# Routing from the logits instead of their exponentials, and layer-norm offsets moved from GpSimd to VectorE

## The chip, the cores and the metric

The kernel runs on one core of one Trainium2 chip. Five engines work in parallel, each through its own queue in order: TensorE (PE in the profile, its weight loads PEld), VectorE (DVE), ScalarE (ACT), GpSimd (POOL) and SyncE (SP), which here only issues DMAs. They wait for each other through semaphores. The metric is the device time of one execution in microseconds.

## What is computed

A transformer block with modulated layer norms (`c`, `wmod`), on 16 batches of 512 tokens with 128 channels: an attention with softmax over each head of q (8 channels) and over the tokens for k, then a mixture of 8 experts of which each token uses 2. Cut to what matters:

```python
h = _layernorm(x) * (1 + ca) + sa
q, k, v = h @ Wq.T + bq, h @ Wk.T + bk, h @ Wv.T + bv
q = softmax(q, axis=-1)            # over the 8 channels of a head
k = softmax(k, axis=-2)            # over the tokens
out = q @ (k.T @ v)                # per head, then a layer norm, Wo, bo
x = x + ga * out
h = _layernorm(x) * (1 + cb) + sb
probs = softmax(h @ router_w)      # 8 experts
top_p, top_e = top_k(probs, 2)
x = x + gb * sum over the two of top_p * (gelu(h @ w_in[e] + b_in[e]) @ w_out[e] + b_out[e])
```

## The kernel before

All five queues are written out by hand, with one loop each over steps b. A step works on several batches at once, at different stages: the experts of batch b+1 (from its second half on; the last ones of batch b before), the attention of b+2, the projections of b+3 and the first layer norm of b+4. In each engine's block a function `step(b)` lists the pieces in their order; a piece starts with the waits for its inputs, and an engine that waits holds up everything behind it. A batch lies in SBUF as 128 partitions by T = 4 tokens by 128 channels. The experts' products `v = u * gate_bc` (`weigh`, 512 columns each) are shared out: experts 1, 3 and 5 to GpSimd, the others to VectorE.

The pieces that matter here, by their lines in the profile:

- First layer norm: `ln1_stats`, `ln1_var` on VectorE give mean and variance (`mv1`), `ve1` (L834) and the negated mean `nm1` (L835). GpSimd's `rstd_L` makes `rstd1` by a power (L328) and the offset `nmr1 = nm1 * rstd1` (L330). ScalarE's `ln1_apply` (L446) uses both. The second norm does the same: L916, L917, L370, L372, and ScalarE's L452 writes `xn2`, which TensorE transposes (L655); ScalarE's L439 and L440 evacuate it to `h2` and `h2_hi`, and GpSimd makes `h2_lo` (L349).
- `k_max`: L839 takes the negated maximum of k over the tokens out of PSUM, L842 makes `kshift` of it and the bias column in `cols`, for ScalarE's exponential (L458).
- `route`: L922 takes the maximum of the 8 logits of each token out of PSUM, L925 subtracts it (`lshift`). ScalarE's `exp_router` (L468) makes `elg`.
- `gates_out`: the two largest of `elg` are found by a maximum (L930) and cut out by a match and replace (L934), 4 times each; `elg - elg_cut` are the chosen ones (L938), times the inverse sum (L936) twice (L943, L944), and the differences (L947). TensorE transposes the result (L666, `gate_turn`); from there it goes over ScalarE (L497) and two DMAs to all partitions as `gate_bc`, for the products.
- VectorE's step ends with `v_bias`, `q_sum` and `route`; the next begins with `q_inv` (L871), `state_out` (`s2T`, L888, after TensorE's L629), `q_norm` (`qn`, L876), `k_inv` and `gates_out`.
- GpSimd's step: `h_low` (L365), `rstd_L`, `rstd_B`, expert 1 (L355), `gated_const` (L334), `residual2` (L359), expert 3, `h2_low` (L349), expert 5, `gated_weight` (L339), `rstd_O` (L344).

Of the kernel before, what the change touches and what calls it, by code (L numbers as in the profile page):

```python
# [27 lines left out]
P = 128  # L28
# [6 lines left out]
def adaln_block(nc, x, Wq, bq, Wk, bk, Wv, bv, Wo, bo, ln_g, ln_b, router_w, w_in, b_in, w_out, b_out, c, wmod, out, gate_scratch, route_scratch):  # L35
# [14 lines left out]
    with ExitStack() as ctx:  # L50
# [3 lines left out]
        def sem(name):  # L54
# [56 lines left out]
        nm1 = sb("nm1", [P, T])  # L111
# [6 lines left out]
        nkmax = sb("nkmax", [P, 1])  # L118
# [23 lines left out]
        nm2 = sb("nm2", [P, T])  # L142
# [6 lines left out]
        lmax = sb("lmax", [P, T])  # L149
        top = sb("top", [P, 4, T, 8])  # L150
        elg_cut = sb("elg_cut", [P, T, NE])
# [3 lines left out]
        einv = sb("einv", [P, T])  # L155
        echosen = sb("echosen", [P, T, NE])
# [29 lines left out]
            "hT_done hhi_ready hlo_ready kT_done kmax_done kshift_ready ek_exp kinv_ready qv_done qb_ready qmax_done qs_ready v_ready "  # L186
# [3 lines left out]
            "h2T_done h2hi_ready h2lo_ready logits_done lmax_done top_done cut_done lshift_ready elg_ready "  # L190
            "esum_done einv_done echosen_done gates_made gate2_ready gateT_done gateT_ready gateTr_ready "
# [106 lines left out]
        def _(pool):  # L298
# [7 lines left out]
            def masks():  # L306
# [8 lines left out]
                pool.memset(top[:, 1:4, :, :], 3.0e38).then_inc(s["const_ready"], 1)  # L315
# [433 lines left out]
        def _(dve):  # L749
# [78 lines left out]
            def ln1_var(n):  # L828
# [81 lines left out]
            def ln2_var(n):  # L910
# [143 lines left out]
```

## Time and profile before

| | before |
|---|---|
| median of 3 runs | 392.79 us (391.56 to 392.8) |
| the profiled execution | 392.8 us, its span 391.1 us |
| TensorE busy | 362.9 us (93%), weight loads 327.3 us (84%) |
| VectorE busy | 282.5 us (72%), 1060 instructions |
| ScalarE busy | 278.5 us (71%) |
| GpSimd busy | 216.8 us (55%), 221 instructions |

The span is the time from the first to the last instruction of the profile. Shares of busy time are averages over all steps; what an operation is worth is read from the waits and from the timelines of one step, which repeats 14 times nearly unchanged. In a timeline row the second number is the duration of the instruction; "xN" stands for N of a kind in a row, merged.

### The profile page before, as it was taken

How to read it: one execution, taken by the hardware profiler on the slowest of the kernel's cores; microseconds unless marked ns; L12 is line 12 of the kernel's file. 1: busy time of each engine (PE TensorE's matmuls, PEld its weight loads, DVE VectorE, ACT ScalarE, POOL GpSimd, SP SyncE). 2: the span in 40 equal slices, each digit the busy share in tenths (PEclk: the TensorE clock that was granted, in tenths of full speed). 3: DMA queues.
4: the chain of work that ended last, by engine and by line, in shares of the span. 5: the costliest groups of instructions: out<-in, count | busy, mean ns of one | idle time of the engine just before them, and what ended most of it. 6: DMA issues, size and time to landing. Idle time of an engine off the chain costs nothing.

```text
span 391.1 us, 8091 instructions
## 1 busy us (share of the span) xinstructions
PE 362.9 (93%) x2502; PEld 327.3 (84%) x2502; DVE 282.5 (72%) x1060; ACT 278.5 (71%) x502; POOL 216.8 (55%) x221
## 2 busy tenths in 40 slices
PE   3657789999999999999999999999999999999995
PEld 3446679889999999899899999898998999988875
DVE  2665586787777888878877778788788787786432
ACT  3333679688787969696887879696969878675740
POOL 2315447373938466483838384664837383754543
PEclk9966579999999999999999999999999999999999
DMA  5570051240706071321606070605224150605061
GB/s 182 151 297 2 0 173 73 80 193 24 247 5 242 29 225 47 157 115 41 231 33 241 3 244 27 240 32 168 106 104 169 38 208 3 217 28 216 32 227 41
DMA packets 18817, 47.83 MB, mean 122 GB/s; under 512 B 2571, under 2 KB 6102, under 8 KB 18518
## 3 DMA queue, kind: packets, MB, share of 16 engines
q1 hardware_dynamic: 18576, 46.90, 33.3%
q8 instruction: 20, 0.33, 0.3%
q10 hardware_dynamic: 198, 0.41, 0.3%
q14 instruction: 23, 0.19, 0.1%
HBM read 42.82 MB, written 4.48 MB: 121 GB/s over the span
## 4 chain that ended last, share of the span: by engine, by line
PE 66%; DVE 9%; issue 6%; DMA 6%; POOL 5%; SPq 4%; ACT 2%; POOLq 0%; DVEq 0%; ACTq 0%
PE pY L684 19%; PE pH L672 6%; PE pH L674 6%; PE pH L673 6%; PE pB L661 4%; PE pQV L641 4%; PE pC L629 4%; PE pC L648 3%; POOL v L355 2%; DVE qn L876 2%; DMA gate_bc<-route_scratch 2%; DMA gates<-gate_scratch 2%; SPq L236 2%; DVE elg_cut L934 2%; PE pA L588 2%
## 5 line engine op out<-in xcount | busy, mean ns | idle before, releaser
L684 PE MATMUL pY<-wout,v 128*128 128x128 f32 x1024 | 128.7, 277 | 1.0 <-DVE v L958 0.7
L684 PEld LDWEIGHTS pY<-wout,v 128*128 128x128 f32 x1024 | 121.7, 193 | 2.2 <-DVE v L958 1.1
L502 ACT ACTIVATE u<-pH,cols 128x512 f32<-128x512 f32 x128 | 86.4, 689 | 49.5 <-PE pH L674 42.8
L344 POOL TENSOR_TENSOR rstd_o<-ve_o,neg_half 128x4 f32<-128x4 f32 x16 | 22.0, 1376 | 104.3 <-DVE ve_o L895 104.3
L958 DVE TENSOR_TENSOR v<-u,gate_bc 128x512 f32<-128x512 f32 x80 | 68.6, 860 | 7.0 <-DMA gate_bc<-route_scratch 3.7
L355 POOL TENSOR_TENSOR v<-u,gate_bc 128x512 f32<-128x512 f32 x48 | 63.7, 1329 | 9.0 <-DMA gate_bc<-route_scratch 9.0
L672 PE MATMUL pH<-h_hi,win_hi 128*128 128x512 f32 x128 | 54.9, 429 | 1.4 <-ACT u L502 1.4
L673 PE MATMUL pH<-h_hi,win_lo 128*128 128x512 f32 x128 | 50.6, 395 | 0.0
L674 PE MATMUL pH<-h_lo,win_hi 128*128 128x512 f32 x128 | 50.5, 394 | 0.0
L349 POOL TENSOR_TENSOR h_lo<-h,h_hi 128x512 fp32r<-128x512 f32 x16 | 22.5, 1405 | 20.2 <-ACT h_hi L440 20.2
L452 ACT ACTIVATE xn<-x_all,nmr,rstd 128x128 f32<-128x128 f32 x64 | 26.2, 482 | 4.5 <-POOL nmr L372 4.5
L847 DVE TENSOR_TENSOR qs<-pQV,bq_bc 128x512 f32<-128x512 f32 x16 | 11.1, 692 | 25.1 <-PE pQV L607 25.1
L672 PEld LDWEIGHTS pH<-h_hi,win_hi 128*128 128x128 f32 x128 | 24.3, 190 | 5.8 <-issue 2.4
L674 PEld LDWEIGHTS pH<-h_lo,win_hi 128*128 128x128 f32 x128 | 24.2, 189 | 5.7
L673 PEld LDWEIGHTS pH<-h_hi,win_lo 128*128 128x128 f32 x128 | 24.4, 190 | 3.4
L446 ACT ACTIVATE xn<-x_all,nmr,rstd 128x128 f32<-128x128 f32 x64 | 26.3, 494 | 0.0
L365 POOL TENSOR_TENSOR h_lo<-h,h_hi 128x512 fp32r<-128x512 f32 x16 | 20.4, 1274 | 8.4 <-ACT h_hi L432 8.4
L902 DVE SCALAR_TENSOR_TENSOR x_all<-pC,rstd_o,x_all 128x128 f32<-128x128 f32 x64 | 18.0, 345 | 8.6 <-PE pC L648 6.7
L359 POOL TENSOR_TENSOR x_all<-x_all,yg 128x512 f32<-128x512 f32 x16 | 21.3, 1332 | 4.4 <-DVE yg L963 4.4
L334 POOL TENSOR_TENSOR x_all<-x_all,gates 128x512 f32<-128x512 f32 x16 | 20.6, 1285 | 5.3 <-DMA gates<-gate_scratch 5.3
L370 POOL TENSOR_TENSOR rstd<-ve,neg_half 128x4 f32<-128x4 f32 x16 | 16.5, 1031 | 10.8 <-DVE nm L917 10.8
L629 PE MATMUL pC<-ek,v_sb 128*128 128x128 f32 x128 | 18.9, 295 | 2.9 <-ACT ek L473 2.9
(151 smaller groups left out, 781.5 us busy)
## 6 DMA issues: line engine op xcount, KB each, us to landing
gate_bc<-route_scratch SPq DMA_DIRECT2D x64, 512.0 KB, 5.7
x_all<-in_L_attn_x SPq DMA_DIRECT2D x16, 256.0 KB, 6.9
out<-x_all SPq DMA_DIRECT2D x16, 256.0 KB, 2.0
gates<-gate_scratch SPq DMA_DIRECT2D x1, 2048.0 KB, 7.1
gb_bc<-gb_scratch SPq DMA_DIRECT2D x1, 1024.0 KB, 4.6
route_scratch<-gateT SPq DMA_DIRECT2D x64, 4.0 KB
win<-in_L_ffn_w_in SPq DMA_DIRECT2D x1, 512.0 KB, 5.6
wout<-in_L_ffn_w_out SPq DMA_DIRECT2D x1, 512.0 KB, 6.9
```

What stands on the lines that cost most here:

```text
L344: pool.tensor_tensor(rstd_o[:, :], ve_o[:, :], neg_half[:, :], ALU.pow).then_inc(s["rstdo_ready"], 1)
L349: pool.tensor_tensor(h2_lo[:, n % 2, :], h2[:, :], h2_hi[:, n % 2, :].bitcast(F32), ALU.subtract).then_inc(s["h2lo_ready"], 1)
L355: pool.tensor_tensor(v[:, e % U, :], u[:, e % U, :], gate_bc[:, b % 2, e, :], ALU.mult).then_inc(s["vp_done"], 1)
L446: act.activation(xn1[:, t, :], x_all[:, n, t, :], ACT.Identity, bias=nmr1[:, t:t + 1], scale=rstd1[:, t:t + 1]).then_inc(s["xn1_ready"], 1)
L452: act.activation(xn2[:, t, :], x_all[:, n, t, :], ACT.Identity, bias=nmr2[:, t:t + 1], scale=rstd2[:, t:t + 1]).then_inc(s["xn2_ready"], 1)
L502: act.activation(u[:, e % U, :], pH[:, e % 2, :], ACT.Gelu_apprx_tanh, bias=cols[:, e:e + 1]).then_inc(s["gelu_done"], 1)
L629: i = mm(pS, v_sb[:, t, :], ek[:, t, :], start=(t == 0), stop=(t == T - 1))
L672: mm(o, win_hi[:, e, :], h2_hi[:, b % 2, :], start=True, stop=False)
L673: mm(o, win_lo[:, e, :], h2_hi[:, b % 2, :], start=False, stop=False)
L674: mm(o, win_hi[:, e, :], h2_lo[:, b % 2, :], start=False, stop=True).then_inc(s["mm1_done"], 1)
L684: i = mm(pY[:, t * P:(t + 1) * P], v[:, e % U, t * P:(t + 1) * P], wout[:, e, :], start=False, stop=(e == NE - 1), skip_group_check=True)
L958: dve.tensor_tensor(v[:, e % U, :], u[:, e % U, :], gate_bc[:, b % 2, e, :], ALU.mult).then_inc(s["v_done"], 1)
```

## The change

Four edits.

1. `k_max`: the maximum is taken without negation, then `kbmax = kmax + bias` and `kshift = bias - kbmax`, two additions of [P, 1] SBUF columns in place of one operation.
2. Layer-norm offsets: `nm1`, `nm2` and GpSimd's two products are gone. VectorE makes `nmr = -mean * rstd` by one operation with two SBUF inputs, in new pieces `ln2_offset` and `ln1_offset`, each behind a wait for GpSimd's rstd.
3. `route` now copies the logits from PSUM to `lg`, takes the 8 sorted values of each token from PSUM (`top`), copies the first two to `top2` (the other six of which hold 3e38), subtracts the largest, and cuts the two largest out of `lg` (`lg_cut`).
4. `gates_out` compares `lg` with `lg_cut` (`chosen`), multiplies by `elg`, then by the inverse sum; the rounded gate is a copy of the gate instead of a second product.

```diff
             def route(n):
                 dve.wait_ge(s["logits_done"], n + 1)
-                logits = pB[:, 0:T * NE].rearrange("p (t e) -> p t e", e=NE)
-                dve.tensor_reduce(lmax[:, :], logits, AX.X, ALU.max).then_inc(s["lmax_done"], 1)
-                dve.wait_ge(s["lmax_done"], n + 1)
-                w(dve, "elg_ready", n)
-                dve.tensor_tensor(lshift[:, :, :], logits, lmax[:, :].unsqueeze(2).to_broadcast([P, T, NE]), ALU.subtract).then_inc(s["lshift_ready"], 1)
+                dve.tensor_copy(lg[:, :, :].rearrange("p t e -> p (t e)"), pB[:, 0:T * NE]).then_inc(s["lg_ready"], 1)
+                for t in range(T):
+                    dve.max(top[:, t, :], pB[:, t * NE:(t + 1) * NE]).then_inc(s["top_done"], 1)
+                dve.wait_ge(s["top_done"], T * n + T)
+                dve.tensor_copy(top2[:, :, 0:2], top[:, :, 0:2]).then_inc(s["top2_done"], 1)
+                dve.wait_ge(s["lg_ready"], n + 1)
+                dve.wait_ge(s["top2_done"], n + 1)
+                dve.tensor_tensor(lshift[:, :, :], lg[:, :, :], top[:, :, 0:1].to_broadcast([P, T, NE]),
+                                  ALU.subtract).then_inc(s["lshift_ready"], 1)
+                for t in range(T):
+                    dve.match_replace(lg_cut[:, t, :], top2[:, t, :], lg[:, t, :], -3.0e38).then_inc(s["cut_done"], 1)
 
             def gates_out(n):
+                dve.wait_ge(s["cut_done"], T * n + T)
+                dve.tensor_tensor(chosen[:, :, :], lg[:, :, :], lg_cut[:, :, :], ALU.not_equal).then_inc(s["chosen_done"], 1)
                 dve.wait_ge(s["elg_ready"], n + 1)
-                for t in range(T):
-                    dve.max(top[:, 0, t, :], elg[:, t, :]).then_inc(s["top_done"], 1)
                 dve.tensor_reduce(esum[:, :], elg[:, :, :], AX.X, ALU.add).then_inc(s["esum_done"], 1)
-                for t in range(T):
-                    dve.wait_ge(s["top_done"], T * n + t + 1)
-                    dve.match_replace(elg_cut[:, t, :], top[:, :, t, 0:2], elg[:, t, :], 0.0).then_inc(s["cut_done"], 1)
...
             def k_max(n):
                 dve.wait_ge(s["kT_done"], n + 1)
-                dve.tensor_reduce(nkmax[:, :], pA[:, :], AX.X, ALU.max, negate=True).then_inc(s["kmax_done"], 1)
+                dve.tensor_reduce(kmax[:, :], pA[:, :], AX.X, ALU.max).then_inc(s["kmax_done"], 1)
                 dve.wait_ge(s["kmax_done"], n + 1)
+                dve.tensor_tensor(kbmax[:, :], kmax[:, :], cols[:, NE:NE + 1], ALU.add).then_inc(s["kbmax_done"], 1)
+                dve.wait_ge(s["kbmax_done"], n + 1)
                 w(dve, "ek_exp", n)
-                dve.tensor_scalar(kshift[:, :], nkmax[:, :], cols[:, NE:NE + 1], cols[:, NE:NE + 1], ALU.subtract, ALU.add).then_inc(s["kshift_ready"], 1)
+                dve.tensor_tensor(kshift[:, :], cols[:, NE:NE + 1], kbmax[:, :], ALU.subtract).then_inc(s["kshift_ready"], 1)
...
+            def ln2_offset(n):
+                dve.wait_ge(s["rstd2_ready"], n + 1)
+                w(dve, "xn2_ready", T * n)
+                dve.scalar_tensor_tensor(out=nmr2[:, :], in0=mv2[:, :, 0], scalar=-1.0, in1=rstd2[:, :],
+                                         op0=ALU.mult, op1=ALU.mult).then_inc(s["nmr2_ready"], 1)
```

What this does to VectorE's queue, at three places of one step. The first is the end of the step, where the routing stands between `q_sum` and the next step's `q_inv`. Before:

```order
L867 TENSOR_REDUCE qsum<-eq 128x64
L922 TENSOR_REDUCE lmax<-pB 128x4
L925 TENSOR_TENSOR lshift<-pB,lmax 128x32
L871 RECIPROCAL qinv<-qsum 128x64
L888 TENSOR_TENSOR s2T<-pC,blockmask 128x128
```

and now (line numbers in these rows are those of the changed kernel):

```order
L873 TENSOR_REDUCE qsum<-eq 128x64
L933 COPY lg<-pB 128x32
L935 MAX top<-pB 128x8 x4
L938 COPY top2<-top 128x4x2
L941 TENSOR_TENSOR lshift<-lg,top 128x32
L944 MATCH_REPLACE lg_cut<-top2,lg 128x8 x4
L877 RECIPROCAL qinv<-qsum 128x64
L894 TENSOR_TENSOR s2T<-pC,blockmask 128x128
```

Two instructions have become five entries with eleven instructions, and the match work stands ahead of `q_inv` and `s2T`. The second place is `gates_out`, between `k_inv` and the copy of the transposed gates. Before:

```order
L930 MAX top<-elg 128x8 x4
L931 TENSOR_REDUCE esum<-elg 128x4
L934 MATCH_REPLACE elg_cut<-top,elg 128x8 x4
L936 RECIPROCAL einv<-esum 128x4
L938 TENSOR_TENSOR echosen<-elg,elg_cut 128x32
L943 TENSOR_TENSOR gate2<-echosen,einv 128x4x8
L944 TENSOR_TENSOR gate2<-echosen,einv 128x4x8
L947 TENSOR_TENSOR gate2<-gate2 128x4x16
```

and now:

```order
L948 TENSOR_TENSOR chosen<-lg,lg_cut 128x32
L950 TENSOR_REDUCE esum<-elg 128x4
L952 TENSOR_TENSOR echosen<-elg,chosen 128x32
L954 RECIPROCAL einv<-esum 128x4
L957 TENSOR_TENSOR gate2<-echosen,einv 128x4x8
L960 CAST gate2<-gate2 128x4x8
L963 TENSOR_TENSOR gate2<-gate2 128x4x16
```

Maxima and replacements are gone from here. The third place is the middle of the step, behind the second layer norm's variance; `v` are the experts' products. Before:

```order
L917 TENSOR_SCALAR nm2<-mv2 128x4
L963 TENSOR_TENSOR yg<-pY,gb_bc 128x512
L958 TENSOR_TENSOR v<-u,gate_bc 128x512
L839 TENSOR_REDUCE nkmax<-pA 128x1
L842 TENSOR_SCALAR kshift<-nkmax,cols 128x1
L847 TENSOR_TENSOR qs<-pQV,bq_bc 128x512
L858 TENSOR_REDUCE qmax<-qs 128x64
L958 TENSOR_TENSOR v<-u,gate_bc 128x512
L862 TENSOR_TENSOR qs<-qs,qmax 128x512
```

and now:

```order
L979 TENSOR_TENSOR yg<-pY,gb_bc 128x512
L974 TENSOR_TENSOR v<-u,gate_bc 128x512
L927 SCALAR_TENSOR_TENSOR nmr2<-mv2,rstd2 128x4
L842 TENSOR_REDUCE kmax<-pA 128x1
L845 TENSOR_TENSOR kbmax<-kmax,cols 128x1
L848 TENSOR_TENSOR kshift<-cols,kbmax 128x1
L853 TENSOR_TENSOR qs<-pQV,bq_bc 128x512
L864 TENSOR_REDUCE qmax<-qs 128x64
L974 TENSOR_TENSOR v<-u,gate_bc 128x512
L836 SCALAR_TENSOR_TENSOR nmr1<-mv1,rstd1 128x4
L868 TENSOR_TENSOR qs<-qs,qmax 128x512
```

`nm2` is gone, the two offsets and one operation of `k_max` have come in. On GpSimd the two offset products behind the powers are gone and nothing else has moved.

## Rows read from the trace of the kernel before

**Rows 1.** waits, whole run: engine, line, releaser: us in total, times, longest
```profile
PEld pB L666 <- DVE gate L947: 5.8, 15, 0.7
```

**Rows 2.** chain of waits, two periods: start us, us, what
```profile
155.89 0.55 DVE elg_cut L934 x4
...
157.30 0.33 PE pB L666
...
178.75 0.33 PE pB L666
```

**Rows 3.** timeline, VectorE: start us, us, engine, line, op, shapes, [idle before <-releaser]
```profile
153.26 0.19 DVE L925 TENSOR_TENSOR lshift<-pB,lmax 128x32 f32<-128x32 f32 x1
153.37 0.54 DVE L871 RECIPROCAL qinv<-qsum 128x64 f32<-128x64 f32 x1
154.57 0.29 DVE L888 TENSOR_TENSOR s2T<-pC,blockmask 128x128 f32<-128x128 f32 x1 [0.67 <-PE pC L629]
154.78 0.68 DVE L876 TENSOR_TENSOR qn<-eq,qinv 128x512 f32<-128x512 f32 x1
...
155.45 0.35 DVE L930 MAX8 top<-elg 128x8 f32<-128x8 f32 x4
...
157.02 0.22 DVE L947 TENSOR_TENSOR gate<-gate 128x64 f32<-128x64 f32 x1
```

**Rows 4.** timeline, GpSimd, around the same step
```profile
154.25 0.46 POOL L339 TENSOR_TENSOR sw_rhs<-wo_gain,gates 128x128 f32<-128x128 f32 x1
...
165.38 1.01 POOL L370 TENSOR_TENSOR rstd<-ve,neg_half 128x4 f32<-128x4 f32 x1 [0.40 <-DVE nm L917]
...
166.62 1.30 POOL L355 TENSOR_TENSOR v<-u,gate_bc 128x512 f32<-128x512 f32 x1
...
170.35 1.28 POOL L355 TENSOR_TENSOR v<-u,gate_bc 128x512 f32<-128x512 f32 x1
173.07 1.45 POOL L349 TENSOR_TENSOR h_lo<-h,h_hi 128x512 fp32r<-128x512 f32 x1 [1.44 <-ACT h_hi L440]
174.48 1.27 POOL L355 TENSOR_TENSOR v<-u,gate_bc 128x512 f32<-128x512 f32 x1
```

**Rows 5.** timeline, VectorE, later in that step
```profile
165.13 0.17 DVE L917 TENSOR_SCALAR nm<-mv 128x4 f32<-128x4 f32 x1
...
165.80 0.68 DVE L958 TENSOR_TENSOR v<-u,gate_bc 128x512 f32<-128x512 f32 x1
...
169.10 0.69 DVE L847 TENSOR_TENSOR qs<-pQV,bq_bc 128x512 f32<-128x512 f32 x1 [1.71 <-PE pQV L607]
...
170.43 1.75 DVE L958 TENSOR_TENSOR v<-u,gate_bc 128x512 f32<-128x512 f32 x1
```

**Rows 6.** timeline, GpSimd, a late step
```profile
342.43 1.75 POOL L355 TENSOR_TENSOR v<-u,gate_bc 128x512 f32<-128x512 f32 x1
```

**Rows 7.** timeline, VectorE, late steps
```profile
342.94 1.78 DVE L862 TENSOR_TENSOR qs<-qs,qmax 128x512 f32<-128x512 f32 x1
...
359.44 1.29 DVE L958 TENSOR_TENSOR v<-u,gate_bc 128x512 f32<-128x512 f32 x2
```

**Rows 8.** one line, L372: duration ns min/median/max, first and last start us
```profile
L372 POOL TENSOR_TENSOR nmr<-nm,rstd x16: 199/202/686, 37.7 to 360.1; 128x4 f32<-128x4 f32 x16
```

**Rows 9.** timeline, ScalarE, the step of rows 3 to 5
```profile
153.96 0.23 ACT L468 ACTIVATE elg<-lshift 128x32 f32<-128x32 f32 x1
...
167.34 1.64 ACT L452 ACTIVATE xn<-x_all,nmr,rstd 128x128 f32<-128x128 f32 x4
```

**Rows 10.** timeline, VectorE, preparation of the weights
```profile
10.62 0.22 DVE L788 TENSOR_SCALAR sw_rhs<-ident 128x128 f32<-128x128 f32 x1
```

**Rows 11.** timeline, GpSimd, near the start and the end
```profile
37.89 1.27 POOL L334 TENSOR_TENSOR x_all<-x_all,gates 128x512 f32<-128x512 f32 x1
...
366.44 1.27 POOL L355 TENSOR_TENSOR v<-u,gate_bc 128x512 f32<-128x512 f32 x1
```

**Rows 12.** timeline, VectorE, the last routing
```profile
366.29 0.19 DVE L922 TENSOR_REDUCE lmax<-pB 128x4 f32<-128x32 f32 x1 [3.74 <-PE pB L661]
```

More of the change, by code:

```diff
@@ L117, in adaln_block @@
         h_lo = sb("h_lo", [P, NTOK], F32R)
-        nkmax = sb("nkmax", [P, 1])
+        kmax = sb("kmax", [P, 1])
+        kbmax = sb("kbmax", [P, 1])
         kshift = sb("kshift", [P, 1])
@@ L148, in adaln_block @@
         h2_lo = sb("h2_lo", [P, 2, NTOK], F32R)
-        lmax = sb("lmax", [P, T])
-        top = sb("top", [P, 4, T, 8])
-        elg_cut = sb("elg_cut", [P, T, NE])
+        lg = sb("lg", [P, T, NE])
+        top = sb("top", [P, T, 8])
+        top2 = sb("top2", [P, T, 8])
+        lg_cut = sb("lg_cut", [P, T, NE])
         lshift = sb("lshift", [P, T, NE])
@@ L155, in adaln_block @@
         einv = sb("einv", [P, T])
+        chosen = sb("chosen", [P, T, NE])
         echosen = sb("echosen", [P, T, NE])
@@ L314, in masks @@
                                    pattern=[[HEAD_DIM, HEADS], [0, HEAD_DIM]], channel_multiplier=-1).then_inc(s["const_ready"], 1)
-                pool.memset(top[:, 1:4, :, :], 3.0e38).then_inc(s["const_ready"], 1)
+                pool.memset(top2[:, :, :], 3.0e38).then_inc(s["const_ready"], 1)
             def gates_loaded():
@@ L367, in rstd_B @@
             def rstd_B(n):
-                pool.wait_ge(s["ve2_done"], 2 * (n + 1))
+                pool.wait_ge(s["ve2_done"], n + 1)
                 w(pool, "xn2_ready", T * n)
                 pool.tensor_tensor(rstd2[:, :], ve2[:, :], neg_half[:, :], ALU.pow).then_inc(s["rstd2_ready"], 1)
-                pool.wait_ge(s["rstd2_ready"], n + 1)
-                pool.tensor_tensor(nmr2[:, :], nm2[:, :], rstd2[:, :], ALU.mult).then_inc(s["nmr2_ready"], 1)
             def step(b):
@@ L832, in ln1_var, with ln1_offset @@
                 dve.wait_ge(s["mv1_done"], T * n + T)
-                w(dve, "nmr1_ready", n)
+                w(dve, "rstd1_ready", n)
                 dve.tensor_scalar(ve1[:, :], mv1[:, :, 1], LN_EPS, None, ALU.add).then_inc(s["ve1_done"], 1)
-                dve.tensor_scalar(nm1[:, :], mv1[:, :, 0], -1.0, None, ALU.mult).then_inc(s["ve1_done"], 1)
+            def ln1_offset(n):
+                dve.wait_ge(s["rstd1_ready"], n + 1)
+                w(dve, "xn1_ready", T * n)
+                dve.scalar_tensor_tensor(out=nmr1[:, :], in0=mv1[:, :, 0], scalar=-1.0, in1=rstd1[:, :],
+                                         op0=ALU.mult, op1=ALU.mult).then_inc(s["nmr1_ready"], 1)
             def k_max(n):
                 dve.wait_ge(s["kT_done"], n + 1)
-                dve.tensor_reduce(nkmax[:, :], pA[:, :], AX.X, ALU.max, negate=True).then_inc(s["kmax_done"], 1)
+                dve.tensor_reduce(kmax[:, :], pA[:, :], AX.X, ALU.max).then_inc(s["kmax_done"], 1)
                 dve.wait_ge(s["kmax_done"], n + 1)
+                dve.tensor_tensor(kbmax[:, :], kmax[:, :], cols[:, NE:NE + 1], ALU.add).then_inc(s["kbmax_done"], 1)
+                dve.wait_ge(s["kbmax_done"], n + 1)
                 w(dve, "ek_exp", n)
-                dve.tensor_scalar(kshift[:, :], nkmax[:, :], cols[:, NE:NE + 1], cols[:, NE:NE + 1], ALU.subtract, ALU.add).then_inc(s["kshift_ready"], 1)
+                dve.tensor_tensor(kshift[:, :], cols[:, NE:NE + 1], kbmax[:, :], ALU.subtract).then_inc(s["kshift_ready"], 1)
             def q_bias(n):
@@ L931, in gates_out @@
                 dve.tensor_reduce(esum[:, :], elg[:, :, :], AX.X, ALU.add).then_inc(s["esum_done"], 1)
-                for t in range(T):
-                    dve.wait_ge(s["top_done"], T * n + t + 1)
-                    dve.match_replace(elg_cut[:, t, :], top[:, :, t, 0:2], elg[:, t, :], 0.0).then_inc(s["cut_done"], 1)
+                dve.wait_ge(s["chosen_done"], n + 1)
+                dve.tensor_tensor(echosen[:, :, :], elg[:, :, :], chosen[:, :, :], ALU.mult)
                 dve.wait_ge(s["esum_done"], n + 1)
@@ L944, in gates_out @@
-                dve.tensor_tensor(gate2[:, :, 1, :].bitcast(F32R), echosen[:, :, :], spread, ALU.mult).then_inc(s["gates_made"], 1)
-                dve.wait_ge(s["gates_made"], 2 * (n + 1))
+                dve.tensor_tensor(gate2[:, :, 0, :], echosen[:, :, :], einv[:, :].unsqueeze(2).to_broadcast([P, T, NE]),
+                                  ALU.mult).then_inc(s["gate_done"], 1)
+                dve.wait_ge(s["gate_done"], n + 1)
+                dve.tensor_copy(gate2[:, :, 1, :].bitcast(F32R), gate2[:, :, 0, :]).then_inc(s["ghi_done"], 1)
@@ L1007, in step @@
                     weigh(b + 1, 0)
+                if has(b + 2):
+                    ln2_offset(b + 2)
                 if has(b + 3):
@@ L1013, in step @@
                     weigh(b + 1, 2)
+                if has(b + 4):
+                    ln1_offset(b + 4)
                 if b == -4:
```

21 lines of the change are left out of this document (6 added, 15 removed).

## The prediction

> **What bounds the kernel now.** I read the waits of TensorE's weight loads first, since TensorE is busy nearly all the time: one wait recurs in every step. The transpose of the gates (L666) waits for VectorE's last gate operation (L947), 15 times, 5.8 us in all [rows 1], 0.39 us a step. The chain of waits then gives the period: that transpose starts at 157.30 and again at 178.75, 21.45 us apart, and the chain reaches it over VectorE, not over TensorE [rows 2]. So the kernel sits where two chains are almost equally long. What VectorE saves here is worth at most 0.39 us a step, then TensorE alone bounds; every microsecond that VectorE is later at this place costs one.
>
> VectorE's timeline ahead of the transpose shows how little room there is [rows 3]. The routing ends with q's reciprocal at 153.91, VectorE idles 0.67 us for the state matmuls, then come s2T (154.57), qn (154.78) and the gate chain from 155.45 to 157.25, 1.80 us long. Starts in that view also price small operations: the next one starts 0.11 us after the start of a 32-column operation that it does not depend on (153.26 to 153.37), and 0.04 us after the end of one that it does (0.19 + 0.04 = 0.23 us).
>
> GpSimd's timeline is the second to look at, for it is not the bound, but works without a gap twice a step [rows 4]: four 512-column operations from 166.62 to 171.63 (L355, L334, L359, L355), and from 173.07 to 176.2 L349, L355 and L339 (the last shown at 154.25 for 0.46 us, one period earlier).
>
> **The port that both engines use.** The trace shows VectorE and GpSimd keeping each other off when both read two SBUF tensors. VectorE's product at 170.43 takes 1.75 instead of 0.69 us and ends 0.55 us after GpSimd's, begun at 170.35, ends [rows 5]. They take turns: at 342.43 GpSimd waits (1.75 instead of 1.28 us) behind a VectorE product, and VectorE's next two-input operation, issued at 342.94, waits until GpSimd is done (1.78 us) [rows 6, 7]. Smallness does not help: GpSimd's 4-column product L372, 0.20 us in the median, takes 0.69 us when VectorE runs two products [rows 6 to 8]. One exception: VectorE's product at 165.80 is not held up though GpSimd's power operation runs from 165.38 to 166.39 [rows 4, 5].
>
> The Trainium skill (SBUF — State Buffer, section "SBUF: two separate sides") states the rule as an exclusive lock held for the whole instruction, and counts among those who take it VectorE operations with two SBUF inputs or in a two-port mode. The 512-column rows agree; the power operation does not, since VectorE was not kept out for its whole duration. With a lock of that whole length the product at 165.80 would have started after 166.39, which the rows exclude, so I let the power operation hold nothing.
>
> **The change, part by part.**
>
> Gate chain (`gates_out`). Gone from it: four maxima (0.35 with a tail of 0.08 that overlaps [rows 3]: 0.27), the four value loads and replacements (0.55 [rows 2]). New: chosen, and a cast that now depends on gate. After: chosen 0.23 to the dependent echosen, +0.11 until the reciprocal, +0.17+0.04 until gate, +0.23 until the cast, +0.20 until the last, which takes 0.22: 1.20 us against 1.80. That is 0.60 us off the critical chain. GpSimd is idle here, so nothing collides.
>
> Routing (`route`). The match work is not gone, it comes earlier, ahead of s2T and qn. New in front of lshift: a copy out of PSUM (0.09 to 0.11), four maxima (0.27), a copy of two columns of each to top2 (0.12 wait, 0.19); behind lshift four replacements (0.55). lshift was read from PSUM and one SBUF tensor and is now read from two SBUF tensors. It is issued while GpSimd runs its fifth product (174.48 to 175.75 [rows 4]). That is what I hold to be decisive.
>
> Offsets. `nm1`, `nm2` vanish (0.17 us each [rows 5], of which I count 0.08, since the next operation does not wait for their end), GpSimd loses two 4-column products, and VectorE makes both offsets itself after a wait for rstd. Behind the wait of ln2_offset stand k_max, q_bias and the rest of VectorE's step; ScalarE's xn (L452, from 167.34 [rows 9]) waits for the result. The wait itself ends in time: with nm2 gone rstd2 is there at about 166.31 instead of 166.39 and the product ahead of it ends at 166.40 instead of 166.48. But GpSimd needs no semaphore after rstd and starts its first product at about 166.28, to 167.58; the offset, with two SBUF inputs, follows at about 167.65. xn starts 0.36 us later, at 167.70. It has cover: its transpose on TensorE comes at 170.7. The delay passes on to h2_hi, and there to GpSimd's L349, 173.07 + 0.36 = 173.43.
>
> Key maximum. One operation becomes two additions with two SBUF inputs each. Each meets one of GpSimd's gapless operations: 168.35 is put off to 169.05, the second to 170.4. q_bias stood idle until 169.10 [rows 5], so it loses 1.3 us. But the product at 170.43 lost 1.07 us to GpSimd before and is now behind it: it ends at 172.42 instead of 172.18. With ln1_offset (0.12) q_sum ends about 0.36 us later, at 174.94; ln1_offset is used at 173.9, later than it is made (172.5).
>
> **The sum for one step**, in the clock of the rows:
> - L349: issued at 173.43, held up by VectorE's product until about 173.65, ends at 174.90; GpSimd's fifth product then runs from 174.86 to 176.13 (before: to 175.75).
> - Copy out of PSUM 174.87, maxima until 175.30, copy to top2 issued at 175.34. A one-source SBUF operation of 128 columns takes 0.22 us [rows 10], one that reads PSUM 0.29 (L888 [rows 3]). I read the difference as twice the reading pace, so through both ports, and take it that top2's copy does so too and waits, to 176.19.
> - GpSimd's L339 (0.46 us) is next in turn, so lshift ends at 176.66 instead of 174.90.
> - Replacements from 176.60, q's reciprocal 177.15, s2T 177.61, qn 177.82, gate chain 178.49, its end 1.21 later, transpose at 179.75.
>
> Against 178.75 that is +1.0 us a step: +1.6 at qn less 0.60 in the gate chain. ScalarE's exponential follows lshift to 176.9 (it was 175.41, from 153.96 [rows 9]), and sw, qT and gateT behind it stay in front of their users by 0.2 us and more. The delay closes the loop, since all that follows hangs on the transpose; it counts in the 14 intervals from gates 0 to gates 14. To this comes the start: at 37.89 GpSimd begins 1.27 us of work [rows 11], now beside the first ln2_offset, for whose result ScalarE and TensorE wait there, +0.9. And the end: the last lmax starts at 366.29 after an idle wait, and GpSimd's product runs from 366.44 to 367.71 [rows 11, 12]; gates end at about 369.65 instead of 368.81, +0.85. Sum: 14 x 1.0 + 0.9 + 0.85 = 15.75. The profiled execution took 392.8 us (391.1 of span and 1.7 around it), which is the median of the three: 408.5 us.
>
> The Trainium skill's page "VectorE: DVE Perf Modes" (section "Mode 2×_2P — use both read ports for one tensor") says that one-source SBUF operations of 32-bit data read their tensor through both ports; with the exclusive lock of the page above, top2's copy would wait as I assume. No row shows such an operation beside a large GpSimd one, so no row decides it.
>
> **The rivals.**
> - *Only two-input operations wait, top2's copy does not.* lshift waits for the fifth product alone and ends at 176.19; everything behind it is 0.47 us earlier, the step +0.5: 14 x 0.52 + 1.75 = 9.0, 401.8 us. For it: two columns are hardly worth a second port. Against it: the doubled pace in [rows 10].
> - *Small operations slip through (faster than before).* If 1 to 32 columns with two SBUF inputs need no turn, lshift ends at 175.1, the replacements and q's reciprocal end at 176.05, just inside the idle 0.67 us, and qn stays at 176.23. Then the gate chain ends 0.6 us sooner, TensorE's wait goes, and the rest is TensorE's own work: -5.8 [rows 1], 387.0 us. It decides as soon as lshift ends before about 175.6. For it: the old kshift, small and beside GpSimd, never waited, but it has one SBUF tensor. Against it: L372 [rows 8].
> - *In between*: turns are given such that lshift ends near 175.7 and gain and loss cancel, 391.6 to 394.
> - *Worse*: VectorE's products later in the step are caught too, another 0.3 us a step, 413 us.
> - That the moved work is not moved is excluded by the instruction order.
>
> **How the numbers follow.** 0.46 for the forecast (408.5), 0.25 for two-input operations alone (401.8), 0.08 for worse (413), 0.07 for in between, 0.14 for the gain (387.0). The range 399 to 412.5 holds the first two with their errors of 0.15 us a step; the gain and the in-between stay out with 0.2. A measurement of this kernel tells 0.3% (1.2 us) from no change. Slower 0.79, the same 0.07, faster 0.14.
>
> **What would show it.** Right: lshift lasts over 0.5 us instead of 0.19 and ends with GpSimd's product or with L339's successor; top2's copy lasts about 0.9 us; one of kbmax and kshift lasts more than 0.5 us; TensorE's wait for the last gate operation grows from 0.39 to over 1 us a step; the period is near 22.45 us. Wrong: all these small operations last under 0.25 us, and the wait at L666 is gone. The forecast also falls if GpSimd's fifth product does not overlap the routing, or if xn's delay reaches TensorE by another way.

## The result

| | before | changed |
|---|---|---|
| median | 392.68 us (391.56 to 392.8) | 402.55 us (401.06 to 402.87) |
| profiled execution | 392.8 us, span 391.1 | 400.12 us, span 398.1 |
| gates 0 to gates 14 (start of their transposes) | 301.70 us | 309.50 us |
| a usual step | 21.45 us | 22.01 us |
| gates 14 to gates 15 | 17.94 us | 18.89 us |

The changed kernel takes 1.0261 times as long, with an interval of 1.0223 to 1.03: slower by 2.6%, as forecast in sign, 6 us less than forecast. The page of the changed kernel begins:

```profile
span 398.1 us, 8137 instructions
...
PE 360.4 (91%) x2502; PEld 323.7 (81%) x2502; DVE 324.8 (82%) x1108; ACT 281.8 (71%) x502; POOL 207.5 (52%) x189
```

TensorE works as long as before; VectorE's busy share has gone from 72% to 82%. Waiting counts as busy here, as the timelines show.

The waits of the whole run (us in total, times, longest), against [rows 1]:

```profile
ACT elg L465 <- DVE lshift L941: 11.3, 16, 2.1
...
PEld pB L663 <- DVE gate L963: 9.6, 16, 1.0
...
PEld pB L658 <- ACT h_hi L437: 8.0, 15, 0.9
```

The weight load for the gates' transpose waits 9.6 instead of 5.8 us, and two others have grown: ScalarE's exponential for lshift (1.0 us before) and the weight load for the logits, for h2_hi (3.4 us before). TensorE's timeline gives the period, against the 157.30 and 178.75 of [rows 2]:

```profile
158.75 0.33 PE L663 MATMUL pB<-ident,gate 128*128 128x128 f32 x1 [0.36 <-DVE gate L963]
...
180.77 0.33 PE L663 MATMUL pB<-ident,gate 128*128 128x128 f32 x1 [0.37 <-DVE gate L963]
```

VectorE's timeline of one step, from s2T over the gate chain to the next routing (compare [rows 3, 5]; durations in us in the second column):

```profile
156.71 0.22 DVE L894 TENSOR_TENSOR s2T<-pC,blockmask 128x128 f32<-128x128 f32 x1
156.85 0.67 DVE L882 TENSOR_TENSOR qn<-eq,qinv 128x512 f32<-128x512 f32 x1
...
157.52 0.17 DVE L948 TENSOR_TENSOR chosen<-lg,lg_cut 128x32 f32<-128x32 f32 x1
...
158.47 0.23 DVE L963 TENSOR_TENSOR gate<-gate 128x64 f32<-128x64 f32 x1
...
167.81 1.25 DVE L927 SCALAR_TENSOR_TENSOR nmr<-mv,rstd 128x4 f32<-128x4 f32 x1
...
169.69 0.62 DVE L845 TENSOR_TENSOR kbmax<-kmax,cols 128x1 f32<-128x1 f32 x1
170.34 1.20 DVE L848 TENSOR_TENSOR kshift<-cols,kbmax 128x1 f32<-128x1 f32 x1
...
172.77 0.68 DVE L974 TENSOR_TENSOR v<-u,gate_bc 128x512 f32<-128x512 f32 x1
...
176.41 0.93 DVE L938 COPY top<-top 128x8 f32<-128x8 f32 x1
177.45 0.33 DVE L941 TENSOR_TENSOR lshift<-lg,top 128x32 f32<-128x32 f32 x1
```

and GpSimd's beside it (compare [rows 4]):

```profile
167.74 1.30 POOL L354 TENSOR_TENSOR v<-u,gate_bc 128x512 f32<-128x512 f32 x1
169.00 1.29 POOL L333 TENSOR_TENSOR x_all<-x_all,gates 128x512 f32<-128x512 f32 x1
170.25 1.27 POOL L358 TENSOR_TENSOR x_all<-x_all,yg 128x512 f32<-128x512 f32 x1
171.47 1.28 POOL L354 TENSOR_TENSOR v<-u,gate_bc 128x512 f32<-128x512 f32 x1
174.82 1.27 POOL L348 TENSOR_TENSOR h_lo<-h,h_hi 128x512 fp32r<-128x512 f32 x1 [2.06 <-ACT h_hi L437]
176.05 1.27 POOL L354 TENSOR_TENSOR v<-u,gate_bc 128x512 f32<-128x512 f32 x1
177.28 0.46 POOL L338 TENSOR_TENSOR sw_rhs<-wo_gain,gates 128x128 f32<-128x128 f32 x1
```

Read the two together, with the wait counted in the duration of the operation that waits. The second offset (L927) is issued at 167.81, just after GpSimd began its product at 167.74, lasts 1.25 us and ends at 169.06, when that product is over (169.04). kbmax ends at 170.31 with the next one (170.29), kshift at 171.54 with the third (171.52). The copy to top2 (L938), eight elements, lasts 0.93 us and ends at 177.34 with the fifth product (177.32). lshift comes in while L338 runs and ends at 177.78, behind it (177.74). All five of these small operations end within 0.05 us after a GpSimd instruction. The product at 172.77, on the other hand, takes its plain 0.68 us: in [rows 5] it took 1.75, and its GpSimd partner is now over before it.

The gate chain, from L948 (157.52) to the end of L963 (158.70), lasts 1.18 us against 1.80 before. So the change shortens what it set out to shorten, and loses more ahead of it.

### The profile page after: what moved, and what is told of

It reads as the page before. It is cut to its first block, busy times and chain, and to the rows that moved or that the text cites. A ratio compares the mean times of both kernels' runs of the same rounds, so it can differ in the third digit from the quotient of the medians.

```text
span 398.1 us, 8137 instructions
## 1 busy us (share of the span) xinstructions
PE 360.4 (91%) x2502; PEld 323.7 (81%) x2502; DVE 324.8 (82%) x1108; ACT 281.8 (71%) x502; POOL 207.5 (52%) x189
## 4 chain that ended last, share of the span: by engine, by line
issue 41%; POOL 29%; DVE 13%; DMA 9%; SPq 4%; ACT 2%; POOLq 1%; PE 1%; DVEq 0%; ACTq 0%
POOL v L354 11%; DMA gate_bc<-route_scratch 4%; POOL x_all L333 4%; POOL x_all L358 3%; POOL h_lo L364 3%; POOL rstd_o L343 2%; DMA route_scratch<-gateT 2%; POOL rstd L329 2%; DMA gates<-gate_scratch 2%; SPq L237 2%; DVE nmr L927 1%; POOL rstd L369 1%; DVE x_all L908 1%; POOL sw_rhs L338 1%; DVE v L974 1%
## 5 line engine op out<-in xcount | busy, mean ns | idle before, releaser
L974 DVE TENSOR_TENSOR v<-u,gate_bc 128x512 f32<-128x512 f32 x80 | 57.7, 723 | 4.8 <-DMA gate_bc<-route_scratch 3.4
L348 POOL TENSOR_TENSOR h_lo<-h,h_hi 128x512 fp32r<-128x512 f32 x16 | 20.3, 1272 | 30.8 <-ACT h_hi L437 30.8
L364 POOL TENSOR_TENSOR h_lo<-h,h_hi 128x512 fp32r<-128x512 f32 x16 | 20.4, 1274 | 8.9 <-ACT h_hi L429 8.9
L658 PEld LDWEIGHTS pB<-rw,h 128*128 128x128 f32 x128 | 16.3, 199 | 9.9 <-ACT h_hi L437 8.0
L333 POOL TENSOR_TENSOR x_all<-x_all,gates 128x512 f32<-128x512 f32 x16 | 20.6, 1286 | 5.6 <-DMA gates<-gate_scratch 5.6
L658 PE MATMUL pB<-rw,h 128*128 128x8 f32 x128 | 17.7, 265 | 5.9 <-ACT h_hi L437 5.8
```

The lines of the kernel that those rows point to most:

```text
L333: pool.tensor_tensor(x_all[:, n, :, :], x_all[:, n, :, :], gates[:, n, 1, :].unsqueeze(1).to_broadcast([P, T, P]), ALU.add).then_inc(s["xg ...
L364: pool.tensor_tensor(h_lo[:, :], h[:, :], h_hi[:, :].bitcast(F32), ALU.subtract).then_inc(s["hlo_ready"], 1)
L658: i = mm(pB[:, t * NE:(t + 1) * NE], h2[:, t * P:(t + 1) * P], rw[:, :], start=True, stop=True)
L974: dve.tensor_tensor(v[:, e % U, :], u[:, e % U, :], gate_bc[:, b % 2, e, :], ALU.mult).then_inc(s["v_done"], 1)
```

## The experiments

Three explanations stood against each other. Theory P: small VectorE operations that need the second way into SBUF (two SBUF inputs, or a copy that reads through two ports) wait for the running GpSimd operation. Theory W: it is the work itself, moved and added ahead of qn. Theory O: it is the offsets, whose wait for rstd puts VectorE behind GpSimd. "Step" below is the usual distance between the gates' transposes. The ratio is to runs of the kernel before on the same chip, with a 95% interval; the runs were made on several chips, on which the kernel before had medians of 392.68 to 392.91 us.

| run | median us | ratio to before | step us |
|---|---|---|---|
| kernel before | 392.68 | 1 | 21.45 |
| changed kernel | 402.55 | 1.0261 (1.0223 to 1.03) | 22.01 |
| a1, routing alone | 399.39 | 1.0145 (1.0108 to 1.0182) | 21.9 |
| a2, offsets alone | 398.06 | 1.012 (1.0084 to 1.0155) | 21.76 |
| a3, k_max alone | 391.17 | 0.9963 (0.9936 to 0.9989) | 21.45 |
| d2, k_max alone again | 392.18 | 0.9987 (0.9973 to 1.0002) | 21.45 |
| a4, changed, routing clear of the port | 393.58 | 1.0027 (0.9995 to 1.0059) | 21.43 |
| b1, clear routing alone | 388.56 | 0.9892 (0.9873 to 0.991) | 21.16 |
| b2, changed, lshift from PSUM | 399.36 | 1.0166 (1.0146 to 1.0187) | 21.86 |
| b3, changed, no copy | 396.49 | 1.0093 (1.0073 to 1.0113) | 21.59 |
| c1, probes (one execution) | 392.75 | | 21.45 |
| d1, clear routing and k_max | 387.39 | 0.9864 (0.9846 to 0.9881) | 21.14 |

**a1, the edits of route and gates_out alone.** The kernel before with the routing of the diff and nothing else of it:

```diff
+                dve.tensor_copy(top2[:, :, 0:2], top[:, :, 0:2]).then_inc(s["top2_done"], 1)
...
+                dve.tensor_tensor(lshift[:, :, :], lg[:, :, :], top[:, :, 0:1].to_broadcast([P, T, NE]), ALU.subtract)
```

> The kernel before with the edits of route and gates_out alone. Theory P (small VectorE operations with two SBUF inputs, or with a two-port copy, wait for GpSimd's running operation): the copy to top2 lasts about 0.8 us and lshift about 0.4 us beside GpSimd's fifth product, the step takes 21.9 instead of 21.45 us, in all +7.5 us, 400 us. Theory W (it is the added and moved work itself, no waiting for GpSimd): copy and lshift last 0.15 to 0.2 us each, the routing is about 0.7 us longer than before, the gate chain 0.6 us shorter, the step within 0.2 us of before, 389 to 395 us. Theory O (the offsets cause the loss, by the wait for rstd): as before or a little faster, 388 to 393 us.

Measured 399.39 us. The two operations in question, over the whole run (min/median/max in ns), and the transposes:

```profile
L928 DVE COPY top<-top x16: 219/768/930, 45.5 to 373.3; 128x8 f32<-128x8 f32 x16
...
L931 DVE TENSOR_TENSOR lshift<-lg,top x16: 191/330/338, 45.8 to 374.3; 128x32 f32<-128x32 f32 x16
```

```profile
159.86 0.33 PE L668 MATMUL pB<-ident,gate 128*128 128x128 f32 x1 [0.46 <-DVE gate L953]
...
181.73 0.33 PE L668 MATMUL pB<-ident,gate 128*128 128x128 f32 x1 [0.46 <-DVE gate L953]
```

The copy lasts 0.77 us in the median, less than in the changed kernel, since it comes in 0.53 us after the start of GpSimd's product (177.55 against 177.02) instead of 0.36: it lasts what is left of it. The time is P's; W would have it at 389 to 395 us, O at 388 to 393.

**a2, the offsets alone.**

```diff
+                dve.scalar_tensor_tensor(out=nmr2[:, :], in0=mv2[:, :, 0], scalar=-1.0, in1=rstd2[:, :],
+                                         op0=ALU.mult, op1=ALU.mult).then_inc(s["nmr2_ready"], 1)
...
-                pool.tensor_tensor(nmr2[:, :], nm2[:, :], rstd2[:, :], ALU.mult).then_inc(s["nmr2_ready"], 1)
```

> The kernel before with the edit of the layer-norm offsets alone. Theory P: the second offset waits for GpSimd's first product (about 1.2 us), ScalarE's xn comes 0.3 us later, and the logits on TensorE with it; since the state matmuls stand behind them, the gate chain comes 0.3 us later: +4 us and under 1 us at the start, about 397 us. Theory W: unchanged within 0.3%. Theory O: nearly the whole loss of the change, 400 us or more.

Measured 398.06 us; the second offset and the transposes:

```profile
L921 DVE SCALAR_TENSOR_TENSOR nmr<-mv,rstd x16: 1212/1249/1259, 37.5 to 366.6; 128x4 f32<-128x4 f32 x16
```

```profile
160.65 0.33 PE L660 MATMUL pB<-ident,gate 128*128 128x128 f32 x1
...
182.40 0.33 PE L660 MATMUL pB<-ident,gate 128*128 128x128 f32 x1
```

A 4-column operation (the first offset, the same operation with no GpSimd instruction beside it, takes 0.15 us in the changed kernel) lasts 1.25 us in every step. The step is 21.75 us, 0.3 longer, as expected; some steps took 22.1 or 22.65, which makes the sum 1 us larger than expected. P's 397 us is the nearest; W (unchanged) and O (400 us or more) are both off. The edit by itself accounts for 5 us, and the routing by itself for 6.5, together for more than the 9.9 of both. In steps: on top of the new routing the offsets cost only 0.11 us (a1 to the changed kernel), not 0.3. The rows show where it goes. Without the offsets GpSimd's h2_low (L351 in a1) comes early enough to meet VectorE's product and lasts 1.44 us; with them it starts 0.31 us later (16.07 instead of 15.76 behind the gates' transpose), when that product is over, and lasts 1.27, so the fifth product ends only 0.14 us later. In a1:

```profile
175.62 1.44 POOL L351 TENSOR_TENSOR h_lo<-h,h_hi 128x512 fp32r<-128x512 f32 x1 [1.45 <-ACT h_hi L442]
```

**a3 and d2, k_max alone.**

```diff
+                dve.tensor_tensor(kbmax[:, :], kmax[:, :], cols[:, NE:NE + 1], ALU.add).then_inc(s["kbmax_done"], 1)
+                dve.wait_ge(s["kbmax_done"], n + 1)
...
+                dve.tensor_tensor(kshift[:, :], cols[:, NE:NE + 1], kbmax[:, :], ALU.subtract).then_inc(s["kshift_ready"], 1)
```

> The kernel before with the edit of k_max alone. Theory P: kbmax and kshift each wait for one of GpSimd's gapless operations (over 0.5 us and over 1 us), but VectorE idled 1.7 us behind them until q_bias, so the time stays within 0.3% of before, 392 to 394 us. Theory W: the same time, but both last under 0.25 us. Theory O: the same as W.

```profile
L843 DVE TENSOR_TENSOR kbmax<-kmax,cols x16: 159/794/801, 18.6 to 338.3; 128x1 f32<-128x1 f32 x16
L846 DVE TENSOR_TENSOR kshift<-cols,kbmax x16: 159/1214/1218, 18.9 to 339.2; 128x1 f32<-128x1 f32 x16
```

Two additions of one column each: 0.79 and 1.21 us in the median, 0.16 in the shortest case. Two microseconds of VectorE's time a step, and the kernel is not slower, since q_bias behind them waited until 169.10 before [rows 5]. The first measurement was even 0.4% under the kernel before, which nothing in its usual steps explains, so it was taken again:

> The kernel of a3 again, with more rounds. Theory P: its step of 21.44 us is that of the kernel before, so it is within 0.3% of it. The rival of d1: about 0.4% faster again, to be looked for ahead of the first gates.

It came out at 0.9987 (0.9973 to 1.0002), not to be told from no change. The idle time covers it. A gain of some 0.1 to 0.3% by another way is not excluded; d1 comes back to it.

**a4, the changed kernel with its routing clear of the port.**

```diff
-                    dve.max(top[:, t, :], pB[:, t * NE:(t + 1) * NE]).then_inc(s["top_done"], 1)
+                    dve.max(top[:, 0, t, :], pB[:, t * NE:(t + 1) * NE]).then_inc(s["top_done"], 1)
...
-                dve.tensor_copy(top2[:, :, 0:2], top[:, :, 0:2]).then_inc(s["top2_done"], 1)
...
-                dve.tensor_tensor(lshift[:, :, :], lg[:, :, :], top[:, :, 0:1].to_broadcast([P, T, NE]), ALU.subtract)
+                dve.tensor_tensor(lshift[:, :, :], pB[:, 0:T * NE].rearrange("p (t e) -> p t e", e=NE), top[:, 0, :, 0:1].to_broadcast([P, T, NE]), ALU.subtract)
...
-                    dve.match_replace(lg_cut[:, t, :], top2[:, t, :], lg[:, t, :], -3.0e38)
+                    dve.match_replace(lg_cut[:, t, :], top[:, :, t, 0:2], lg[:, t, :], -3.0e38)
```

> The changed kernel with its routing kept clear of the shared port: the maxima are written in the old layout of top beside the 3e38 rows, so no copy to top2 is needed, and lshift reads the logits from PSUM, so it has one SBUF input. All else as changed, offsets and k_max included. Theory P: lshift lasts 0.19 us, the loss of the routing goes (about -0.75 us a step against the changed kernel), the later h2_hi keeps about 0.3 us of the gain: a step of 21.3 to 21.5 us, 390 to 395 us. Theory W: a saving of the copy's own 0.2 us a step at most, 399 to 402 us. Theory O: 401 us or more.

```profile
L938 DVE TENSOR_TENSOR lshift<-pB,top x16: 190/192/193, 46.2 to 371.4; 128x32 f32<-128x32 f32 x16
```

lshift lasts 0.19 us again, and the time falls to 393.58 us, 9 us below the changed kernel (1.0027 against 1.0261 as ratios), although the same maxima, the same replacements and the same copy out of PSUM stand at the same place. That rules out W: what was taken away is one 8-element copy, 0.2 us a step by itself and 3 us in 14 steps, and one operand's memory. It rules out O too, since the offsets are still there. What remains is the logits' wait for h2_hi, in six steps of the middle:

```profile
PEld pB L657 <- ACT h_hi L436: 3.2, 6, 0.9
```

0.5 us a step, as in the changed kernel; the wait for the gates is not among the answers any more. That wait was 0.60 us a step in the changed kernel (9.6 us in 16), and the step has become 0.58 us shorter.

**b1, the clear routing alone.** The kernel before with a4's routing; offsets and k_max as before.

> The kernel before with the new routing, kept clear of the shared port as in a4 (no copy to top2, lshift reads PSUM), and neither the offsets nor k_max changed. Theory P: the gate chain is 0.6 us shorter and the routing costs no waiting, TensorE no longer waits for the last gate operation (0.39 us a step gone): a step of about 21.1 us, 386 to 389 us. Theory W: the longer routing eats it, 391 to 394 us.

```profile
PEld pB L662 <- ACT h_hi L441: 1.3, 7, 0.2
```

```profile
156.73 0.27 PE L667 MATMUL pB<-ident,gate 128*128 128x128 f32 x1
...
177.89 0.27 PE L667 MATMUL pB<-ident,gate 128*128 128x128 f32 x1
```

388.56 us, 1.1% faster than before. The logits' wait is back at 0.2 us, the gates' wait is gone, and the step is 21.16 us. The idea of the change, to find the two experts from the logits while the exponential is under way, shortens the gate chain by its 0.6 us and, as long as nothing of it needs the port, the step by 0.29: from there on TensorE does not wait for the gates any more.

**b2, lshift alone moved back to PSUM, and b3, the copy alone taken away.** In b2 the changed kernel's lshift reads `pB` instead of `lg`; in b3 there is no copy to top2 (layout as in a4), and lshift reads `lg`.

```diff
 b2
-                dve.tensor_tensor(lshift[:, :, :], lg[:, :, :], top[:, :, 0:1].to_broadcast([P, T, NE]), ALU.subtract)
+                dve.tensor_tensor(lshift[:, :, :], pB[:, 0:T * NE].rearrange("p (t e) -> p t e", e=NE), top[:, :, 0:1].to_broadcast([P, T, NE]), ALU.subtract)
 b3
-                dve.tensor_copy(top2[:, :, 0:2], top[:, :, 0:2]).then_inc(s["top2_done"], 1)
```

> The changed kernel with one operand changed: lshift reads the logits from PSUM, the copy to top2 stays. Theory P: the copy still lasts about 0.9 us and ends with GpSimd's product, lshift 0.19 instead of 0.33 us and not behind L338; a step 0.15 us shorter than the changed kernel's 22.0, 399 to 401.5 us. Theory W: as the changed kernel, 402 to 403 us.

> The changed kernel without the copy to top2 (maxima in the old layout of top), lshift with two SBUF inputs as changed. Theory P: lshift itself now waits for GpSimd's fifth product, lasts about 0.9 us and ends some 0.4 us earlier than in the changed kernel; a step of about 21.6 us, 396 to 399 us. Theory W: 0.2 us a step saved, 399 to 400 us, lshift 0.19 us.

```profile
L938 DVE COPY top<-top x16: 211/930/942, 46.0 to 372.3; 128x8 f32<-128x8 f32 x16
...
L941 DVE TENSOR_TENSOR lshift<-pB,top x16: 191/192/193, 46.3 to 373.4; 128x32 f32<-128x32 f32 x16
```

```profile
L938 DVE TENSOR_TENSOR lshift<-lg,top x16: 228/954/960, 46.0 to 369.3; 128x32 f32<-128x32 f32 x16
```

In b2 the copy still lasts 0.93 us, lshift 0.19; in b3 there is no copy, and now it is lshift that lasts 0.95 us. The wait passes to whichever operation comes first. Both times are P's: 399.36 and 396.49 us. Taking away one of the two brings 0.15 or 0.42 us a step, and the two add up to the 0.58 us of a4.

**c1, which operations wait.** The kernel before with one idle operation a step behind kshift, beside GpSimd's first product, of a kind that changes from step to step; its results are not used.

```diff
                     k_max(b + 3)
+                    probe(b + 3)
...
+                if kind == 0:
+                    i = dve.tensor_tensor(dump[:, 0:1], probe_a[:, 0:1], probe_b[:, 0:1], ALU.add)
...
+                elif kind == 3:
+                    i = dve.tensor_copy(dump[:, 0:1], probe_a[:, 0:1])
```

> The kernel before with one idle operation behind kshift in each step, where GpSimd is in its first product and VectorE has 1.7 us of idle time; the kind changes from step to step. Theory P: a sum of two SBUF columns (1 wide) and of two 32-wide tiles last 0.4 us or more, like kbmax; a copy of 4 x 2 elements and one of 32 too, since they read through both ports; a copy of one column, a product of 32 columns by a column scalar and a match and replace last their plain 0.15 to 0.2 us. Theory W: all under 0.25 us. The time as before within 0.5%.

One of each kind (each kind came two or three times; the forms give partitions x elements; L850 and L852 have two SBUF inputs, L854 copies 4 x 2 elements, L857 one, L859 32, L861 multiplies 32 columns by a column scalar):

```profile
103.34 0.62 DVE L859 COPY dump<-probe_a 128x32 f32<-128x32 f32 x1
...
167.67 0.61 DVE L850 TENSOR_TENSOR dump<-probe_a,probe_b 128x1 f32<-128x1 f32 x1
...
189.88 0.37 DVE L852 TENSOR_TENSOR dump<-probe_a,probe_b 128x32 f32<-128x32 f32 x1
...
211.14 0.63 DVE L854 COPY dump<-probe_a 128x8 f32<-128x8 f32 x1
...
232.60 0.14 DVE L857 COPY dump<-probe_a 128x1 f32<-128x1 f32 x1
...
275.49 0.63 DVE L861 TENSOR_SCALAR dump<-probe_a,probe_b 128x32 f32<-128x32 f32 x1
...
297.01 0.15 DVE L863 MATCH_REPLACE8 dump<-probe_a,probe_b 128x8 f32<-128x8 f32 x1
```

392.75 us, as before. Two SBUF inputs of one column: 0.61 us. Copies of 4 x 2 and of 32 elements: 0.63. A copy of one column: 0.14. The match and replace: 0.15 with its value load before it. The four that last 0.61 to 0.63 us end within 0.05 us after GpSimd's product beside them. All this is as expected but for L861 and, by a little, L852. The miss is L861: a one-source operation of 32 columns with a column scalar waits as well, 0.63 us both times. The prediction's own sentence on one-source SBUF operations covers it; c1's expectation left it out. L852 lasted 0.37 us, just under the 0.4 expected: it came in later in a product that ended at 190.20, and ended at 190.25 (the other one of its kind beside a product lasted 0.53 us). Why the old kshift, also with column scalars, never waits (0.27 us in every step here) is not shown for certain; it is one column wide, like the copy that does not wait.

**d1, the fastest version.** The clear routing of b1 with the k_max edit of a3; against a4 only the offsets differ.

> The clear routing of b1 and the k_max edit together, offsets as before: against a4 only the offsets differ. Theory P: the waits of kbmax and kshift stay covered by the idle time before q_bias, so the step is that of b1, 21.15 us, and the time that of b1, 388 to 389 us; the distance to a4 (393.6) is the offsets' price where the routing is out of the way, 0.3 us a step. A rival: k_max by itself brings something (a3 measured 0.4% under the kernel before), then 386.5 to 387.5 us.

387.39 us, step 21.14. The step is b1's, but the time lies in the rival's range (386.5 to 387.5), not in P's. The ratios of b1 and d1 overlap (0.9873 to 0.991 and 0.9846 to 0.9881), and d2 by itself was not to be told from no change; so k_max is neutral or gains up to 0.3%, and which of the two stays open. Against a4 the medians differ by 6.2 us: 14 times the 0.29 us of the step, the offsets' price as in a2, are 4.1, and the other 2 us no kept trace explains. The two profiled executions do not serve for it. That of a4 took 396.85 us, 3.3 above a4's median, and has most of its excess in one early stretch: it reached gates 1 at 75.29 us (b1 71.11, d1 70.00), with a granted clock of 0.82 from 50 to 76 us against 0.93 in b1 and 0.97 in d1.

## Why the prediction was right, and where its sizes were off

*The place.* Right: VectorE's chain to the gates' transpose sets the period, before and after. The sign given for it did not come in full: TensorE's wait there was to grow from 0.39 to over 1 us a step and grew to 0.60. The rest of the lost time shows at the logits, whose weight load waits for h2_hi 8.0 us instead of 3.4 in the whole run, about 0.3 us more a step; that is the offsets' part.

*The port.* Right for the copy, for kbmax and kshift and for the offset; lshift waits too, but only a little. The copy lasts 0.93 us (about 0.9 forecast), kbmax and kshift 0.62 and 1.20, the offset 1.25. lshift was to last over 0.5 us and lasts 0.33. That GpSimd's power operation (`pow`, 4 columns) keeps nobody waiting stays right; it can itself be late beside VectorE's product:

```profile
162.37 0.69 DVE L974 TENSOR_TENSOR v<-u,gate_bc 128x512 f32<-128x512 f32 x1
...
167.21 0.68 DVE L974 TENSOR_TENSOR v<-u,gate_bc 128x512 f32<-128x512 f32 x1
```

```profile
162.51 1.43 POOL L343 TENSOR_TENSOR rstd_o<-ve_o,neg_half 128x4 f32<-128x4 f32 x1 [6.78 <-DVE ve_o L901]
...
166.76 1.01 POOL L369 TENSOR_TENSOR rstd<-ve,neg_half 128x4 f32<-128x4 f32 x1 [0.62 <-DVE ve L922]
```

The product at 167.21 begins in the middle of the power operation of 166.76 and takes its plain 0.68 us; the power operation at 162.51, issued behind a product of VectorE's that has begun, takes 1.43 instead of 1.01. In c1 a sum of two 32-column SBUF tiles began at 37.67 inside the power operation of 36.94 to 37.95 and took 0.18. The Trainium skill (SBUF — State Buffer, "SBUF: two separate sides") states an exclusive lock; the rows shown agree for GpSimd's elementwise operations of 128 and 512 columns, and not for the power operation. The Trainium skill (VectorE: DVE Perf Modes, "Mode 2×_2P — use both read ports for one tensor") has a copy within SBUF read through both ports, and c1 agrees with what follows from it: 0.63 us for 4 x 2 elements. The part of the prediction that no row of before could decide was decided for it.

*The gate chain.* 1.20 us forecast, 1.18 measured.

*The step.* +1.0 us forecast, +0.56 measured. This is the main term of the sum that was mis-sized (14 times 0.44 is 6.2 us, and the whole forecast lies 6 us too high), and 0.41 of the missing 0.44 us can be followed, counting from the end of the gate chain (157.24 before, 158.70 after). The forecast had GpSimd's fifth product end 18.89 us behind it; it ended 18.62 behind (177.32). The forecast let L349 be held up by VectorE's product at its start; in the run VectorE's product was over at 174.74 (the one issued at 174.05, 0.69 us long) and L348 started at 174.82 with its plain 1.27 us. VectorE was ahead of the forecast because I had let each small VectorE operation push GpSimd's next one back: counted as above, the offset ended 0.10 us, kbmax 0.20 and kshift 0.32 us earlier than forecast (10.36 against 10.46, 11.61 against 11.81, 12.84 against 13.16). The three GpSimd operations beside the offset, kbmax and kshift last 1.30, 1.29 and 1.27 us, no more than before. The next 0.07 us: L339 was to start only after the copy; in the run L338 starts at 177.28, as if there were no copy, and lshift is 0.33 us long instead of waiting a whole 0.46. The last 0.07 us is s2T, which no longer waits for its input and has its successor start 0.14 instead of 0.21 us behind it (156.71 to 156.85).

*The offsets.* xn was to start 0.36 us later; it started 10.39 us behind the gate chain's end (169.09) against 10.10 before, 0.29. It passes on to h2_hi and to the logits, as forecast; a2 prices that at 0.3 us a step where the routing is the old one.

*Start and end.* Forecast +0.9 and +0.85. The end: gates 14 to 15 took 0.95 longer, but in the profiled executions most of that was won back behind gates 15 (22.23 us from there to the end of the span before, 21.45 now), where the last products wait for `gate_bc`: the first of VectorE's that waits for it began 7.07 us after the copy of the transposed gates before (369.54 to 376.61), 6.29 now (377.32 to 383.61). From gates 14 to the end the changed kernel is only 0.17 us longer; the forecast took it that a delay of the last gates reaches the end whole. The start: GpSimd's work beside the first offset, [rows 11], and ScalarE's xn behind it, in the changed kernel:

```profile
36.28 1.27 POOL L333 TENSOR_TENSOR x_all<-x_all,gates 128x512 f32<-128x512 f32 x1
```

```profile
37.61 1.65 ACT L449 ACTIVATE xn<-x_all,nmr,rstd 128x128 f32<-128x128 f32 x4 [5.82 <-DVE nmr L927]
```

xn begins 1.33 us after L333 instead of 0.08 (37.97 against 37.89), so the offset's wait is there, and from L333 to gates 0 it takes 11.98 us instead of 11.34: 0.64 of the 0.9. Gates 0 come 0.97 us earlier all the same (48.26 against 49.23), because this execution reached L333 1.6 us sooner. Its granted clock over the first 48 us was 0.86, that of before 0.77; whether that is the reason is not shown, and b2, with 0.91, reached gates 0 only at 49.46. The profiled execution took 2.4 us less than the changed kernel's median; the medians differ by 9.9 us where the profiles differ by 7.3.

*The rivals.* The time is nearest to the rival in which the copy does not wait (401.8 us). Its mechanism is false: the copy waits. The agreement is chance: its sum carries the mis-sizing above and leaves out the copy's wait, and the two cancel. The rival with the gain (387.0) was false for the changed kernel; b1 and d1, where the routing does not wait, come near its time: 388.6 and 387.4 us.

## What to carry to other kernels

Where VectorE and GpSimd work side by side, count a small VectorE operation not by its size but by its operands: with two SBUF inputs, or as a multi-element copy from SBUF to SBUF, it lasts until GpSimd's running product, sum or difference is over, up to 1.25 us here. Reading one operand from PSUM, or laying a tile out so that the copy is not needed, took 9 us out of this kernel with no more work taken out than a copy of 0.2 us a step. Work that is moved off a critical chain must be looked at where it arrives: beside GpSimd, the same edit lost 1.5% and, clear of it, gained 1.1%.

## What the runs showed of the hardware that was not expected

- A copy of 4 x 2 elements waits for GpSimd (0.63 us in c1, up to 0.94 in b2); a copy of one column does not (0.14, twice), nor does a match and replace (0.15, twice).
- A product of 32 columns by a column scalar from SBUF waits too (0.63 us, twice).
- GpSimd's power operation of 4 columns (1.01 us) does not keep a VectorE operation with two SBUF inputs waiting (0.68 us for 512 columns, 0.18 for 32).
- A VectorE operation of one to 32 columns that takes its turn between two GpSimd operations does not lengthen the second in the records (1.27 to 1.30 us), while one of 512 columns does ([rows 6]).
- The granted clock of the first 48 us differed from one profiled execution to the next, from 0.77 (before) over 0.81 (b1) to 0.91 (b2); these are executions of different kernels, and the time of gates 0 does not follow it.
